# VectorE's fp8 rounding divided between two steps, and the router's exponential moved between the shared units

## The reference

```python
ln_out = _ln(hidden_states, ln_w, ln_b)
q = _ln(_fp8_linear_pertensor(ln_out, wq, ...))      # 16 heads of 128; k: 8 groups; v: 8 groups, no norm
qx = _ln(_fp8_linear_pertensor(ln_out, wqx, ...))
kx, vx = jnp.split(jnp.einsum('bsi,oi->bso', cond, w_kv_x), 2, axis=-1)
core = _gqa(q, k, v)                                 # softmax over the 64 tokens of a sequence
xout = _gqa(qx, _ln(kx), vx)
cat = jnp.concatenate([core, xout], axis=-1)
...   # cat / smooth, clipped to +-448, rounded to fp8 e4m3, times wproj; times tanh(g_xattn), added to x
...   # layer norm, router over 16 experts, top 2, softmax weights over the chosen two;
...   # shared expert + sum of the two experts, each silu(x Wg) * (x Wu) Wd; times tanh(g_ffn), added
```

## Time and profile before

| | us |
|---|---|
| median of 3 runs | 453.41 (452.15 to 453.7) |
| the profiled execution | 453.45 |
| its span, first to last instruction | 451.7 |
| PE busy in it | 393.8 (87%) |
| DVE busy | 365.4 (81%) |
| ACT busy | 292.3 (65%) |
| POOL busy | 282.9 (63%) |

### The profile page before, as it was taken

How to read it: one execution, slowest core, us unless ns; L and a number is a source line. 1 busy time by engine, 2 the same in 40 slices (tenths; PEclk the granted TensorE clock), 3 DMA queues, 4 the chain that set the end, 5 groups by cost and what they waited for, 6 DMA issues and landing times.

```text
span 451.7 us, 11249 instructions
## 1 busy us (share of the span) xinstructions
PE 393.8 (87%) x3626; PEld 290.1 (64%) x3626; DVE 365.4 (81%) x836; ACT 292.3 (65%) x620; POOL 282.9 (63%) x379
## 2 busy tenths in 40 slices
PE   0677899999989989989998998998999496999960
PEld 0444567666757757656775675766687395899950
DVE  5967989999999999999999999999988761433337
ACT  3598888777767857767776775786963213666520
POOL 2079677875876778677687677855674740366640
PEclk9999999999999999999999999999988588999995
DMA  8950929999940000000000000000194213344317
GB/s 212 265 198 2 155 34 299 254 294 270 257 135 0 0 0 0 0 0 0 0 0 0 0 0 0 0 1 2 39 429 176 96 56 95 109 130 146 92 49 238
DMA packets 34621, 45.57 MB, mean 101 GB/s; under 512 B 2970, under 2 KB 32031, under 8 KB 33696
## 3 DMA queue, kind: packets, MB, share of 16 engines
q1 hardware_dynamic: 26368, 35.34, 26.4%
q0 software_dynamic: 6944, 9.46, 9.5%
q10 hardware_dynamic: 1280, 0.41, 0.4%
HBM read 28.21 MB, written 24.19 MB: 116 GB/s over the span
## 4 chain that ended last, share of the span: by engine, by line
PE 34%; DVE 31%; issue 14%; ACT 10%; POOL 6%; DMA 2%; ACTq 1%; POOLq 1%; SPq 0%; DVEq 0%
PE proj_ps L969 6%; DVE st L1378 6%; DVE yv L1405 3%; PE proj_ps L961 3%; PE out_ps L1031 3%; PE pv_ps L1021 3%; PE proj_ps L1137 3%; PE score_ps L998 3%; PE headT_ps L1137 3%; DVE ys L1344 2%; DVE reg L1389 2%; PE headT_ps L987 2%; DVE mx L1386 2%; DVE sm L1395 2%; ACT kT L744 2%
## 5 line engine op out<-in xcount | busy, mean ns | idle before, releaser
L969 PE MATMUL proj_ps<-arena 128*128 128x512 f16 x384 | 99.7, 382 | 3.0 <-DVE arena L1370 3.0
L1378 DVE BATCH_NORM_STATS2 st<-rot 128x6 f32<-128x256 f32 x192 | 72.4, 419 | 5.7 <-ACT rot L709 4.4
L571 POOL TENSOR_TENSOR rot<-rot,cw 128x512 f32<-128x512 f32 x64 | 67.3, 1072 | 2.5
L730 ACT ACTIVATE rot<-rot,cw 128x128 f32<-128x128 f32 x128 | 40.9, 391 | 32.7 <-POOL cw L565 32.7
L709 ACT ACTIVATE rot<-proj_ps 128x512 f32<-128x512 f32 x96 | 56.2, 585 | 8.1 <-PE proj_ps L969 6.5
L577 POOL TENSOR_TENSOR reg<-reg,rinv 128x512 f32<-128x512 f32 x32 | 33.5, 1047 | 35.3 <-DVE rinv L1398 35.3
L969 PEld LDWEIGHTS proj_ps<-arena 128*128 (+1 forms) x384 | 34.8, 98 | 29.4 <-issue 3.8
L641 POOL DMA_INDIRECT ybuf<-arena,bslot x31 | 30.6, 985 | 32.4 <-DVE bslot L1584 15.4
L961 PE MATMUL proj_ps<-arena 128*128 128x512 f16 x192 | 46.7, 379 | 0.6 <-POOL arena L527 0.6
L987 PE MATMUL headT_ps<-idf,rot 128*128 128x128 f32 x256 | 39.0, 275 | 8.3 <-ACT kT L744 8.3
L987 PEld LDWEIGHTS headT_ps<-idf,rot 128*128 128x128 f32 x256 | 30.0, 141 | 16.5 <-issue 9.9
(11 more groups left out here) (228 smaller groups left out, 874.1 us busy)
## 6 DMA issues: line engine op xcount, KB each, us to landing
zbuf<-fill SPq DMA_DIRECT2D x1, 16576.5 KB, 65.4
arena<-in_wffn SPq DMA_DIRECT2D x4, 1536.0 KB, 13.4
arena<-zbuf SPq DMA_DIRECT2D x30, 128.5 KB
wkv_stage<-in_wkvN SPq DMA_DIRECT2D x1, 2048.0 KB, 15.3
wp_sb<-in_wpT POOLq DMA_DIRECT2D x1, 2048.0 KB, 16.6
wp_sb<-ybuf SPq DMA_DIRECT2D x8, 256.0 KB, 5.5
xs<-in_x SPq DMA_DIRECT2D x2, 512.0 KB, 5.2
vv<-in_wqN POOLq DMA_DIRECT2D x1, 1024.0 KB, 12.4
```

The costliest lines, as they stand in the source:

```text
L571: gp.tensor_tensor(r, r, cw[:, 4 * i:4 * i + 4].unsqueeze(2).to_broadcast([P, 4, D]), ALU.mult)\
L730: ins = act.activation(r, r, ACT.Copy, scale=cw[:, h:h + 1])
L969: mm = pe.matmul(ps, lhs, w[kind][:, ch, 512 * b:512 * b + 512], start=(k == 0), stop=(k == 3))
L1378: ins = ve.bn_stats(st[:, 4 * i + h:4 * i + h + 2, :].rearrange("p h s -> p (h s)"), raw[c % 2][i][:, h * D:(h + 2) * D].rearrange("p (h d ...
```

## The change

Step n of DVE's loop now begins with the add of unit n-4 and has its subtract between the softmax maximum and the softmax subtraction of unit n-2. `over_smooth` becomes one operation over both banks and stands ahead of the third statistics. Clip, absolute value and magnitude of unit n-3 end the step, and in c = 1 they alternate with the same three of the inputs. PE's `output` of unit n-4 moves from ahead of the third projection to behind the first head transpose. `route_shift` moves ahead of unit 3, `router_exp` ahead of the silu of unit 5 with two table loads, `route_weights` ahead of `unit_hidden` of unit 6.

```diff
-        pv_ps = [bank("pv_ps0"), bank("pv_ps1")]
+        pv_both = ctx.enter_context(nc.psum_tensor("pv_ps", [P, 1024], F32))
+        pv_ps = [pv_both[:, 0:512], pv_both[:, 512:1024]]
...
-            for u in range(2, FIRST):
+            for u in range(2, FIRST - 1):
                 unit_silu(u)
+            act.preload_act_table_set("natural_log_exp_and_others")
+            router_exp()
+            act.preload_act_table_set("silu_and_others")
+            unit_silu(FIRST - 1)
...
-            act.preload_act_table_set("natural_log_exp_and_others")
-            router_exp()
...
                     values(n - 3, (c - 3) % NU)
-                if live(n, 4) and proj:
-                    output(n - 4, c, t - 1)
...
                     head_transposes(n - 1, before, 0)
-                if live(n, 4) and not proj:
+                if live(n, 4):
                     output(n - 4, c, t - 1)
...
             def over_smooth(w, u, y=yv):
                 ve.wait_ge(pv_done, w + 1)
-                y3 = y[:, :].rearrange("p (h t) -> p h t", t=P)
-                for b in range(2):
-                    ins = ve.tensor_tensor(y3[:, :, b * S:(b + 1) * S],
...
+                ve.tensor_tensor(y[:, :].rearrange("p (h b s) -> p b h s", b=2, s=S),
+                                 pv_both[:, :].rearrange("p (b h s) -> p b h s", b=2, s=S),
+                                 smi[:, 8 * u:8 * u + 8].unsqueeze(1).unsqueeze(3).to_broadcast([P, 2, 8, S]),
+                                 ALU.mult).then_inc(y_done, 1)
...
+            def values_grid(w, u):
+                ve.wait_ge(big_done, w + 1)
+                if isinstance(w, int):
+                    ge(ve, op_done, w - 1)
+                else:
+                    ve.wait_ge(score_done, w + 3)
+                ve.tensor_tensor(catq[u % 2], ys[:, :], ym[:, :], ALU.subtract).then_inc(catq_done, 1)
...
             def step(t, c):
+                if live(n, 4):
+                    values_big(n - 4)
                 if proj:
                     stats(n, c, 0)
...
                 if attend:
-                    softmax_in(n - 2, c % 2)
+                    softmax_max(n - 2)
+                if live(n, 4):
+                    values_grid(n - 4, c)
+                if attend:
+                    softmax_sub(n - 2, c % 2)
                 if proj:
                     stats(n, c, 1)
...
                     softmax_sum(n - 2, c % 2)
+                if live(n, 3):
+                    over_smooth(n - 3, (c - 3) % NU)
                 if proj:
                     stats(n, c, 2)
...
+                spread = c == 1 and live(n, -NU)
                 if live(n, 3):
-                    over_smooth(n - 3, (c - 3) % NU)
+                    values_clip(n - 3)
+                if spread:
+                    inputs_clip(t + 1)
                 if live(n, 3):
-                    quantise(n - 3, (c - 3) % NU)
-                if proj and c == 1 and live(n, -NU):
-                    inputs_magnitude(t + 1)
+                    values_abs(n - 3)
+                if spread:
+                    inputs_abs(t + 1)
+                if live(n, 3):
+                    values_mag(n - 3)
+                if spread:
+                    inputs_mag(t + 1)
...
             block_table()
+            route_shift()
             unit_hidden(3)
-            for u in range(4, FIRST + 1):
+            for u in range(4, FIRST):
                 unit_out(u - 2)
                 unit_hidden(u)
+            unit_out(FIRST - 2)
+            route_weights()
+            unit_hidden(FIRST)
             unit_out(FIRST - 1)
-            route_shift()
...
-            route_weights()
```

More of the change, by code:

```diff
@@ L1328, in _, with inputs_clip, inputs_abs @@
                 fold_low(j)
[L1330 to L1350, removed]
+            def inputs_clip(T):
                 ve.wait_ge(xin_done, T + 1)
                 ve.tensor_scalar(xin[:, :], xin[:, :], FP8_MAX, -FP8_MAX, ALU.min, ALU.max).then_inc(xclip_done, 1)
+            def inputs_abs(T):
                 ve.wait_ge(xclip_done, T + 1)
@@ L1365, in _ @@
                              .to_broadcast([P, 4, HC, P]), ALU.mult).then_inc(xin_done, 1)
-            inputs_magnitude(0)
+            inputs_clip(0)
+            inputs_abs(0)
+            inputs_mag(0)
             ve.wait_ge(xmag_done, 1)
@@ new lines, in values_big @@
+            def values_big(w, y=yv):
+                ve.wait_ge(mag_done, w + 1)
+                ve.tensor_tensor(ys[:, :], y[:, :], ym[:, :], ALU.add).then_inc(big_done, 1)
+            def values_grid(w, u):
[5 more added lines that the diff above has]
+                ve.tensor_tensor(catq[u % 2], ys[:, :], ym[:, :], ALU.subtract).then_inc(catq_done, 1)
@@ new lines, in quantise, with softmax_max, softmax_sub @@
+            def quantise(w, u, y=yv):
+                values_clip(w, y)
+                values_abs(w, y)
+                values_mag(w)
+                values_big(w, y)
+                values_grid(w, u)
+            def softmax_max(w):
+                ve.wait_ge(score_done, w + 1)
+                ve.tensor_reduce(mx[:, :], score_ps[:, :].rearrange("p (g t) -> p g t", t=S), AX.X,
+                                 ALU.max).then_inc(max_done, 1)
+            def softmax_sub(w, s):
+                ve.wait_ge(max_done, w + 1)
+                ge(ve, probn_done, w - 1)
+                ve.tensor_tensor(prob[s].rearrange("p (g t) -> p g t", t=S),
+                                 score_ps[:, :].rearrange("p (g t) -> p g t", t=S),
+                                 mx[:, :].unsqueeze(2).to_broadcast([P, 8, S]),
+                                 ALU.subtract).then_inc(sub_done, 1)
@@ L1606, in _ @@
                 last - 2: lambda: [rows_scale(0), index_words(0)]})
+            values_big(last - 4)
             rows_in(1)
-            softmax_in(last - 2, 0)
+            values_grid(last - 4, 0)
+            softmax_max(last - 2)
+            softmax_sub(last - 2, 0)
             over_smooth(last - 3, 1)
@@ L1611, in _ @@
             softmax_sum(last - 2, 0)
-            quantise(last - 3, 1, by_pool=True)
-            softmax_in(last - 1, 1)
+            values_clip(last - 3)
+            values_abs(last - 3)
+            values_mag(last - 3)
+            softmax_max(last - 1)
+            softmax_sub(last - 1, 1)
             route_best(0)
```

26 lines of the change are left out of this document (10 added, 16 removed).

## The result

| us | before | changed |
|---|---|---|
| median of the runs | 453.12 (452.15 to 453.7, 4 runs) | 439.27 (438.61 to 440.28, 4 runs) |
| profiled execution | 453.45 | 438.61 |
| its span | 451.7 | 436.8 |
| loop tile | 37.40 | 35.65 |

A forecast was written before the change was run, and what follows sets the result against it. DVE was taken to bound the loop at 37.40 us a tile, PE 1.7 behind. Six loop tiles -6.9, tiles 0 and 7 and last units -0.2, router +0.55: -6.55 on 453.45 gives 446.9, range 442 to 456.5.

The forecast's parts named there:

- What bounds the kernel: Loop tiles: DVE sets the 37.40 us tile, PE needs about 35.7, POOL and ACT have 10 us of slack.
- (a): Loop, DVE: 18 dependent neighbours a tile are parted, each saving 0.11 us, 1.98 us a tile.
- (b): Loop, DVE: one over_smooth for two saves 0.06 us a step, 0.24 a tile (-0.3 to +0.4).
- (c): Loop, c = 1: inputs' absolute value and magnitude fall from 1.15 to 0.43 us each, clear of POOL's products; gain 1.44.
- (d): Loop, DVE: the moved grid subtract waits for POOL's bank products, 2.4 us a tile (0 to 4.2); DVE then needs 36.1.
- 0.15 for coupling: Loop tile: DVE's 36.1 and PE's 35.7 are so close that they wait for each other; 0.15 us added, tile 36.25.
- my first rival: Loop: PE becomes the bound at 35.7 a tile if subtracts meet POOL's products in half the steps; 443.6 us, chance 0.22.
- (e): Loop, PE: output moves 1.3 us later, its subtract ends about 1.4 plus its wait later; slack 0.5 to 1.5, no cost.
- (f): Tiles 0 and 7 and the last units: savings and subtract waits together give -0.2 us, between -2 and +1.
- The router: Units behind the loop: silu of unit 5 and its DMA 0.6 us late, +0.55 (0 to +0.9); weights leaving the end gain nothing.

The follow-up runs named there:

- the first single edit: Kernel before with over_smooth, still two operations, ahead of the third statistics and nothing else: 451.06 us, ratio 0.9847, tile 36.23.
- the kernel with less TensorE: Changed kernel without 2 of the 6 matmuls in each context projection (output not the reference's): 438.36 us, ratio 0.9663 to the kernel before.
- the loop part alone: Changed kernel with the router's three steps put back, run twice: 446.08 us, ratio 0.9782, then 439.42, ratio 0.9697, to the kernel before.

## Why the prediction was wrong, step by step

**What bounds the kernel**: right in the kernel before, though DVE's slices at 9 tenths run from the seventh to the 29th and the sixth shows 8; and PE's need, read as 35.7 from two steps of its timeline, was measured at 35.65.

**(a) dependent neighbours**: right. The spacings of independent operations fell to 0.33 to 0.36 for 0.41 to 0.43, and the first single edit gives its 0.44 once the 0.72 is taken off. The Trainium skill, VectorE: DVE Perf Modes, section The DRAIN you can't avoid, says that a semaphore between chained operations costs nothing extra. These runs don't agree: an operation that waits for the one before it costs 0.11 more than one that doesn't. Undoing five of the eighteen pairs (the trios in turn) brought the need without waits from 33.1 to 35.71 - 2.13 = 33.6, 0.1 a pair.

**(b) one over_smooth**: 1.17 to 1.20 for 1.27, 0.10 to 0.07 each where I took 0.06 (1.21 in the kernel with this edit alone).

**(c) the inputs' operations**: right, 1.44. The clip took 0.41 for 0.43, 0.08 more.

**(d) the grid subtract's waits, with the sum of 36.1 and its 0.15 for coupling**: this is the step that failed in the loop. I laid 2.4 us of waits on the tile as a fixed price and had VectorE set it at 36.25. The subtracts wait 1.1 in the changed kernel, VectorE has 0.9 left over in which it waits for ACT, and TensorE sets 35.65. That 2.4 is close to VectorE's waits at its own pace (2.6 in the kernel with less TensorE) is in part luck: 1.7 of them are at the subtract, the other 0.9 at an add that I had not counted. And the need beneath was 33.1, not 33.7: 0.2 from (b) and the clip, the rest from three gaps in the kernel before, 0.09 to 0.14 longer than others of their kind, that I had counted as work. So VectorE alone would set 35.67, not 36.1, with TensorE's 35.65 beside it. At TensorE's pace the waits shrink, so nothing of (d) reaches the tile, and the 0.15 for coupling isn't there either. The tile is that of my first rival (35.7), which had 0.22, but not by its condition: the subtract meets a product in all four steps, and waits each time only for the part of it that is left. The Trainium skill, SBUF — State Buffer, section Who interferes with whom, says that a VectorE instruction with two SBUF inputs contends with a GpSimd instruction that reads SBUF. These runs agree, and the subtract waits 0.15 to 0.57 in the changed kernel, not the 1.0 of a whole product each time.

**(e) PE's output**: its cost of nothing was right; the late place turned out to be needed.

**(f) tiles 0 and 7 and the last units**: this step failed too, and by as much: -0.2 forecast, while tile 7 and the way to the row transposes gave -1.46 - 1.62 = -3.1, and the +0.93 at the start is not in the second profile. I laid (d)'s 0.7 on each of these steps as well, and in tile 7 PE is busy 36.30 of 36.59 us. The two operations of the earlier trace rows run ahead of POOL's products now, as foretold:

```profile
298.44 0.17 DVE L1268 TENSOR_TENSOR tw<-tw 128x6 f32<-128x6 f32 x1
298.63 0.17 DVE L1513 SCALAR_TENSOR_TENSOR tn<-tmv,tw 128x6 f32<-128x6 f32 x1
...
299.05 2.36 POOL L572 TENSOR_TENSOR rot<-rot,cw 128x512 f32<-128x512 f32 x2
```

**The router**: the 0.55 was wrong, by its mechanism, and no run shows it. I followed unit 3, the silu of unit 5 and the DMA behind it. The DMA waited for POOL's scatters, as it did in every run: SP's DMA came 1.9 to 3.9 after the last scatter's end, while the last scatter ended 5.8 after the row positions each time. At the end, that the transfer is late next was right where ACT had no long wait ahead of the last silu; where it had one, the weights cost about 1.1 (first sum 6.0 to 6.3 after the start of the last scatter of block rows, as in the kernel before, against 4.7 to 5.1 elsewhere). In the changed kernel the last scatter ended at 361.17 and SP's DMA followed 1.90 later, as before; only ACT's own came 0.56 behind it, held by the exponential's second table load and the silu:

```profile
359.21 0.42 DVE L1607 TENSOR_TENSOR arena<-headT_ps,arena 128x256 f32<-128x256 f32 x1
...
363.07 4.17 SPq L479 DMA_DIRECT2D arena<-zbuf  x4
...
361.25 1.28 ACT L881 ACT_TABLE_LOAD   x1
362.64 0.39 ACT L831 ACTIVATE arena<-headT_ps 128x256 f32<-128x256 f32 x1
363.63 0.37 ACTq L887 DMA_DIRECT2D arena<-zbuf  x1
```

Together: the loop's six tiles gave 9.5 instead of 6.9 (2.6 of the missing), the rest behind and before it 5.4 instead of a loss of 0.35 (5.7), by the spans of two executions. Of the last part 3.1 is (f). The other 2.3 hang on these two executions as far as the runs tell: 1.1 is the wait ahead of the last silu, which made the weights late in the kernel before, 0.8 is TensorE's clock on the way to the positions, and +0.93, -0.63 and -0.46 lie within what profiles of like kernels differ by.

## What to carry to other kernels

When two engines are within a few per cent of each other, work out both needs and ask what the slower one's waits become at the other's pace: waits for a shared port are not a fixed price, they shrink when the engine is no longer the one that sets the pace. A late result costs nothing until its reader comes, so compare the two in each step and not the sums over a tile: 0.9 us of lost time cost 0.3 in one place, 1.5 us cost 0.06 in others. Before a chain is priced, look for what its last member waits for in the trace: two DMAs on two queues that go out in the same instant have a releaser in common, and that was the one to shorten. When two needs agree to 0.02, cutting one alone shows nothing for it; only the cut of both shows that there are two.

## What was not expected of the hardware

A meeting of VectorE and GpSimd has a sharp edge: the inputs' operation of 0.43 takes 0.43 when it starts 0.12 ahead of GpSimd's product and 1.15 when it comes 0.24 behind the product's start, so single edits gave 0.72 more than their own price. TensorE's granted clock rose from 0.50 to 1.00 sooner in one profile than in another of the same 54 operations, and that alone was 0.8 us. ACT had waits of 2.6 to 3.9 us put down to no engine of the core, one or two an execution, all among the blocks and the last units: in the profile of the kernel before, in all eight of the first and third batch of experiments, in none of the second and fourth, and not in the changed kernel's first profile but in its second. So they go with the chip or the session and not with the kernel; their cause is open. The two profiles of the loop part alone differ by 4.3 us in span (441.5 and 437.2), 3.6 of it behind the first block transposes.
